# The attributes' bias added by VectorE, epsilon as a third triple of the statistics, a centred first matrix, spare rows by a maximum

## What is computed

```
h    = max(layernorm(x), 0)                       # eps 1e-5, no gamma
xn   = layernorm(h) * g1 + b1
msg  = relu(xn[src] + edge_attr)                  # one row per edge
aggr = segment_sum(msg, dst)                      # one row per node
u    = (1 + eps_gin) * xn + aggr
x2   = h + relu(u @ Wg1 + bg1) @ Wg2 + bg2
f    = gelu((layernorm(x2) * g2 + b2) @ Wf1 + bf1) @ Wf2 + bf2
out  = x + x2 + f
```

## Time and profile before

| | us |
|---|---|
| median of three runs | 1241.77 |
| profiled execution, its own time | 1243.35 |
| profiled execution, span | 1241.6 |
| busy: TensorE, VectorE, ScalarE, GpSimd | 1099.0, 1118.4, 999.1, 939.4 |
| same over 140 to 1150 us | 954.90, 968.17, 875.25, 814.47 |

### The profile page before, as it was taken

How to read it: one execution, slowest core, us unless ns; L and a number is a source line. 1 busy time by engine, 2 the same in 40 slices (tenths; PEclk the granted TensorE clock), 3 DMA queues, 4 the chain that set the end, 5 groups by cost and what they waited for, 6 DMA issues and landing times.

```text
span 1241.6 us, 28921 instructions
## 1 busy us (share of the span) xinstructions
PE 1099.0 (89%) x7264; PEld 921.0 (74%) x7264; DVE 1118.4 (90%) x5523; ACT 999.1 (80%) x2354; POOL 939.4 (76%) x698
## 2 busy tenths in 40 slices
PE   0257899999899999999899899999999999999988
PEld 0235688778788787788788787778778778787877
DVE  2888899999899999999899998999999999999842
ACT  0258789889888888989888888989889889979864
POOL 4488688878787887878787888888788788885630
PEclk9967999999999999999999999999999999999989
DMA  5879944444444444444444444544454454443220
GB/s 118 322 233 327 342 112 121 113 108 121 110 110 122 108 111 121 109 109 123 107 109 117 115 111 104 124 105 111 111 121 111 107 123 113 112 100 83 52 54 34
DMA packets 111491, 157.15 MB, mean 127 GB/s; under 512 B 24592, under 2 KB 51640, under 8 KB 111367
## 3 DMA queue, kind: packets, MB, share of 16 engines
q1 hardware_dynamic: 73606, 130.31, 32.8%
q0 software_dynamic: 37760, 25.66, 14.8%
HBM read 91.26 MB, written 64.61 MB: 126 GB/s over the span
## 4 chain that ended last, share of the span: by engine, by line
DVE 58%; issue 14%; POOL 11%; PE 9%; ACT 2%; DMA 1%; DVEq 1%; SPq 0%; ACTq 0%; POOLq 0%
DVE n_stat L635 12%; DVE n_mom L640 5%; DVE n_in L826 5%; POOL aggr_sums L480 5%; DVE e_stat L635 4%; DVE n_relu L645 4%; DVE e_match L740 4%; DVE n_out L833 3%; DVE n_x L811 3%; DVE n_zg L816 3%; DVE n_x2b L845 3%; PE p_f L892 3%; PE p_out L936 3%; POOL e_x L427 2%; DVE e_sum L798 2%
## 5 line engine op out<-in xcount | busy, mean ns | idle before, releaser
L480 POOL DMA_INDIRECT aggr_sums<-e_merged,e_index x196 | 326.5, 1666 | 81.9 <-issue 57.3
L936 PEld LDWEIGHTS p_out<-wf,n_act 128*128 128x128 f32 x3136 | 365.6, 192 | 3.5
L936 PE MATMUL p_out<-wf,n_act 128*128 128x128 f32 x3136 | 365.9, 275 | 0.0
L503 ACT ACTIVATE n_act<-p_f,bf1e_col 128x512 f32<-128x512 f32 x392 | 264.1, 674 | 18.1 <-PE p_f L892 17.5
L427 POOL DMA_INDIRECT e_x<-in_x,e_cols x196 | 216.4, 1104 | 71.9 <-issue 53.7
L494 ACT ACTIVATE n_z<-n_relu,n_shift,n_rstd 128x128 f32<-128x128 f32 x392 | 161.6, 483 | 127.9 <-DVE n_shift L664 127.4
L892 PE MATMUL p_f<-n_z2T_high,wf_low 128*128 128x512 f32 x392 | 190.6, 486 | 62.6 <-DVE n_z2T_low L678 35.9
L440 POOL TENSOR_TENSOR n_rstd<-n_var,minus_half 128x8 f32<-128x8 f32 x98 | 196.7, 2007 | 5.3 <-DVE n_var L657 5.3
L892 PEld LDWEIGHTS p_f<-n_z2T_high,wf_low 128*128 128x128 f32 x392 | 74.9, 191 | 164.0 <-ACT n_act L503 114.8
L446 POOL TENSOR_TENSOR n_rstd<-n_var,minus_half 128x4 f32<-128x4 f32 x98 | 103.5, 1056 | 119.8 <-DVE n_var L855 118.7
L635 DVE BATCH_NORM_STATS2 n_stat<-n_x 128x6 f32<-128x128 f32 (+1 forms) x784 | 168.9, 276 | 0.0
(11 more groups left out here) (91 smaller groups left out, 1997.3 us busy)
## 6 DMA issues: line engine op xcount, KB each, us to landing
n_x<-in_x SPq DMA_DIRECT2D x97, 256.0 KB, 2.9
n_aggr<-aggr_sums SPq DMA_DIRECT2D x97, 256.0 KB
out_dram<-n_out SPq DMA_DIRECT2D x97, 256.0 KB
aggr_sums<-zeros SPq DMA_DIRECT2D x13, 1024.0 KB, 8.3
e_dst<-in_dst_rows SPq DMA_DIRECT2D x49, 256.0 KB, 3.7
e_attr<-in_attr SPq DMA_DIRECT2D x48, 256.0 KB, 2.8
aggr_sums<-zeros SPq DMA_DIRECT2D x6, 2048.0 KB, 13.5
e_x<-in_x,e_cols POOLq DMA_INDIRECT x196, 2.8
```

Of the source, the lines that this page charges most:

```text
L480: nc.gpsimd.indirect_dma_start(out=aggr, out_offset=bass.IndirectOffsetOnAxis(ap=e_index[0:r, s, j:j + 1], axis=0), in_=e_merged[0:r, s, j ...
L503: nc.scalar.activation(n_act[:, k, :, 0:b.rows], p_f[k % 2][:, :, 0:b.rows], ACT.Gelu, bias=bf1e_col[:, k:k + 1]).then_inc(s_act, 1)
L936: last = nc.tensor.matmul(p_out[0:b.rows, j, :], n_act[:, k, j, 0:b.rows], wf2[:, k, :], start=False, stop=(k == KF - 1), skip_group_check ...
```

## The change

1. The addition of b1 to the attributes moves from GpSimd to VectorE (`add_b1`), behind the match matrix at the end of each step with half 0. SyncE's next load of attributes still waits for the same semaphore, now raised by VectorE.
2. The statistics' tiles have nine numbers for a row. The last three are a constant third triple (0, 0, 128 x 1e-5), written at the start by six memsets, so that `bn_aggr` over nine numbers gives the variance with 1e-5 in it. `first_variance` and `n_var2` go; `variance` writes into the moments, and GpSimd reads the moments with a step of two. Three of the five kinds of `bn_aggr` read nine numbers (the first and the third layernorm of a node, the first of an edge), two still read six.
3. Wf1 times g2 gets the mean over its 128 rows subtracted (one more matmul, one more VectorE subtraction, once), so the third layernorm no longer needs its mean: `shift2` goes, and ScalarE scales without a shift.
4. `e_toward` goes: `e_extra` is the spare row or 0, and `e_index` is the maximum of it and the destination.

```
                 if (b := node(1)) is not None:
-                    nc.gpsimd.tensor_tensor(n_rstd[0:r, s], n_var[0:r, s],
+                    nc.gpsimd.tensor_tensor(n_rstd[0:r, s], n_mom[0:r, s, :, :, 1],
...
                 if (b := node(4)) is not None:
-                    pool.wait_ge(s_var2, b.at + 1)
-                    nc.gpsimd.tensor_tensor(n_rstd2[0:r, s], n_var2[0:r, s], minus_half[0:r, 0:J],
+                    pool.wait_ge(s_mom2, b.at + 1)
+                    nc.gpsimd.tensor_tensor(n_rstd2[0:r, s], n_mom2[0:r, s, :, 1], minus_half[0:r, 0:J],
                                             ALU.pow).then_inc(s_rstd2, 1)
                 if 0 in halves and (c := edge(2)) is not None:
-                    if c.is_number(0):
-                        pool.wait_ge(s_edge_param, 16 * len(EDGE_PARAMS))
-                    pool.wait_ge(q_attr[s], 16 * (c.uses(3) + 1))
-                    reached(pool, s_esum, c.at - 2)
-                    nc.gpsimd.tensor_tensor(e_attrb[0:r, s], e_attr[0:r, s], b1_row[0:r],
-                                            ALU.add).then_inc(s_eattrb, 1)
                     pool.wait_ge(s_evar, c.at + 1)
-                    nc.gpsimd.tensor_tensor(e_rstd[0:r, s], e_var[0:r, s, 1], minus_half[0:r, 0:J],
+                    nc.gpsimd.tensor_tensor(e_rstd[0:r, s], e_mom[0:r, s, 1, :, 1], minus_half[0:r, 0:J],
                                             ALU.pow).then_inc(s_erstd, 1)
...
                 if (b := node(4)) is not None:
-                    act.wait_ge(s_shift2, b.at + 1)
+                    r = b.rows
+                    act.wait_ge(s_rstd2, b.at + 1)
                     reached(act, s_tz2, b.at - 1)
-                    per_row(n_z2[:, b.slot(2)], n_x2[:, b.slot(3)], n_rstd2[:, b.slot(6)],
-                            n_shift2[:, b.slot(6)], b.rows).then_inc(s_z2, 1)
+                    for j in range(J):
+                        last = nc.scalar.activation(n_z2[0:r, b.slot(2), j, :], n_x2[0:r, b.slot(3), j, :],
+                                                    ACT.Identity, scale=n_rstd2[0:r, b.slot(6), j:j + 1])
+                    last.then_inc(s_z2, 1)
...
+            nc.vector.memset(mean_of[:], 1.0 / D).then_inc(s_ones, 1)
+            for of in (e_stat[:, :, 0], n_stat[:, :, 0], n_stat2[:]):
+                nc.vector.memset(of[:, :, :, 6:8], 0.0).then_inc(s_stat_eps, 1)
+                nc.vector.memset(of[:, :, :, 8:9], EPS * D).then_inc(s_stat_eps, 1)
...
+                dve.wait_ge(s_wf1, 1)
+                dve.wait_ge(s_wf1_mean, 1)
+                nc.vector.tensor_tensor(wf1g[:], wf1g[:], p_f[1][:].rearrange("p j q -> p (j q)"),
+                                        ALU.subtract).then_inc(s_wf1, 1)
+                dve.wait_ge(s_wf1, 2)
+                nc.vector.tensor_copy(wf1_high[:], wf1g[:]).then_inc(s_wf1, 1)
                 dve.wait_ge(s_b1g, 1)
-                dve.wait_ge(s_wf1, 2)
+                dve.wait_ge(s_wf1, 3)
                 nc.vector.tensor_tensor(wf1_low[:], wf1g[:], wf1_high[:], ALU.subtract).then_inc(s_wf1, 1)
                 dve.wait_ge(s_b2f, 1)
...
-            def moments(to, of, rows, done):
+            def moments(to, of, width, rows, done):
+
                 for j in range(J):
-                    last = nc.vector.bn_aggr(to[0:rows, j, :], of[0:rows, j, :])
+                    last = nc.vector.bn_aggr(to[0:rows, j, :], of[0:rows, j, 0:width])
                 last.then_inc(done, 1)
...
-            def first_variance(var, mom, rows, done):
-
-                nc.vector.tensor_scalar(var[0:rows, 0, :], mom[0:rows, 0, :, 1], EPS, None, ALU.add).then_inc(done, 1)
-
-            def second_variance(var, mom, rows, first, at, done):
-
-
-                dve.wait_ge(first, at + 1)
-                nc.vector.scalar_tensor_tensor(var[0:rows, 1, :], var[0:rows, 0, :], EPS,
+            def variance(mom, rows, done):
+
+                nc.vector.scalar_tensor_tensor(mom[0:rows, 1, :, 1], mom[0:rows, 0, :, 1], EPS,
                                                mom[0:rows, 1, :, 1], ALU.mult, ALU.add).then_inc(done, 1)
 
...
-            def shift2(node):
-                if (b := node(4)) is not None:
-                    r, s = b.rows, b.slot(6)
-                    dve.wait_ge(s_rstd2, b.at + 1)
-                    nc.vector.scalar_tensor_tensor(n_shift2[0:r, s], n_mom2[0:r, s, :, 0], -1.0, n_rstd2[0:r, s],
-                                                   ALU.mult, ALU.mult).then_inc(s_shift2, 1)
...
                     dve.wait_ge(s_estat, c.at + 1)
                     nc.vector.tensor_copy(e_dstf[0:r, s], e_cols[0:r, s, 1, :]).then_inc(s_ecopy, 1)
-                    moments(e_mom[:, s, 0], e_stat[:, s, 0], r, s_emom)
-
-                    dve.wait_ge(s_ecopy, c.at + 1)
-                    nc.vector.tensor_tensor(e_toward[0:r, s], spare[0:r], e_dstf[0:r, s],
-                                            ALU.subtract).then_inc(s_etoward, 1)
+                    moments(e_mom[:, s, 0], e_stat[:, s, 0], STAT, r, s_emom)
                     dve.wait_ge(s_emom, c.at + 1)
...
                     shift(node)
-                shift2(node)
                 z2_low(node)
-                first_variance_of(node)
                 if c is not None:
 
 
                     dve.wait_ge(q_dst[s], 16 * (c.uses(3) + 1))
+                    dve.wait_ge(s_ecopy, c.at + 1)
...
-                second_variance_of(node)
+                variance_of(node)
+
+            def add_b1(c):
+
+                if c is not None:
+                    r, s = c.rows, c.slot(3)
+                    if c.is_number(0):
+                        dve.wait_ge(s_edge_param, 16 * len(EDGE_PARAMS))
+                    dve.wait_ge(q_attr[s], 16 * (c.uses(3) + 1))
+                    reached(dve, s_esum, c.at - 2)
+                    nc.vector.tensor_tensor(e_attrb[0:r, s], e_attr[0:r, s], b1_row[0:r],
+                                            ALU.add).then_inc(s_eattrb, 1)
...
-                    nc.vector.scalar_tensor_tensor(e_extra[0:r, s], e_count[0:r, s], 1.5, e_toward[0:r, s],
+                    nc.vector.scalar_tensor_tensor(e_extra[0:r, s], e_count[0:r, s], 1.5, spare[0:r],
                                                    ALU.is_gt, ALU.mult).then_inc(s_eextra, 1)
-                    moments(e_mom[:, s, 1], e_stat[:, s, 1], r, s_emomu)
+                    moments(e_mom[:, s, 1], e_stat[:, s, 1], 6, r, s_emomu)
                     relu_moments(node)
                     if not (c.fixed and c.k < 3):
                         dve.wait_ge(q_scatter[s], SCATTERED * c.uses(3))
                     dve.wait_ge(s_eextra, c.at + 1)
                     nc.vector.tensor_tensor(e_index[0:r, s], e_dstf[0:r, s], e_extra[0:r, s],
-                                            ALU.add).then_inc(s_eindex, 1)
-                    dve.wait_ge(s_emomu, c.at + 1)
-                    first_variance(e_var[:, s], e_mom[:, s], r, s_evar0)
+                                            ALU.max).then_inc(s_eindex, 1)
...
                     relu_moments(node)
-                shift2(node)
                 z2_low(node)
-                first_variance_of(node)
                 if c is not None:
-                    second_variance(e_var[:, s], e_mom[:, s], r, s_evar0, c.at, s_evar)
-                second_variance_of(node)
+                    dve.wait_ge(s_emomu, c.at + 1)
+                    variance(e_mom[:, s], r, s_evar)
+                variance_of(node)
                 if ending is not None:
...
-                    moments(n_mom[:, b.slot(6), 0], n_stat[:, b.slot(6), 0], b.rows, s_nmom)
+                    moments(n_mom[:, b.slot(6), 0], n_stat[:, b.slot(6), 0], STAT, b.rows, s_nmom)
                 if (b := fifth) is not None:
                     r, s = b.rows, b.slot(6)
                     dve.wait_ge(s_stat2, b.at + 1)
                     nc.vector.tensor_tensor(n_x2b[0:r, s], n_x2[0:r, b.slot(3)], n_x[0:r, s],
                                             ALU.add).then_inc(s_x2b, 1)
-                    moments(n_mom2[:, s], n_stat2[:, s], r, s_mom2)
...
-                if (b := fifth) is not None:
-                    r, s = b.rows, b.slot(6)
-                    dve.wait_ge(s_mom2, b.at + 1)
-                    nc.vector.tensor_scalar(n_var2[0:r, s], n_mom2[0:r, s, :, 1], EPS, None,
-                                            ALU.add).then_inc(s_var2, 1)
                 if 0 in halves or not halves:
                     first_half(edge(1), node)
+                    if 0 in halves:
+                        add_b1(edge(2))
                 if 1 in halves:
                     second_half(edge(1), edge(2), node)
...
+            pe.wait_ge(s_wf1, 1)
+            pe.wait_ge(s_ones, 3)
+            nc.tensor.matmul(p_f[1][:], mean_of[:], wf1g[:], start=True, stop=True).then_inc(s_wf1_mean, 1)
             pe.wait_ge(s_bias, 1)
-            pe.wait_ge(s_wf1, 3)
+            pe.wait_ge(s_wf1, 4)
```

(22 more changed lines are left out.)

34 lines of the change are left out of this document (15 added, 19 removed).

## The result

The changed kernel takes 1193.67 us as the median of four runs (1191.93 to 1194.49), the kernel before 1241.97 (1239.85 to 1242.43) beside it. The profiled execution took 1193.22 us (before 1243.35), so 50.1 us are to be found in the two traces.

The account below looks back on a forecast made before the run. VectorE was taken as the bound, busy 968.2 of 1010 us in the middle; -26.0 + 29.4 + 3.1 - 21.7 - 3.0 - 2.4 = -20.6 us, from 1243.35 to 1222.8, stated as 1222; own ends 1208 and 1236, range up to 1240.

Parts of the forecast that it names:

- small instructions removed: VectorE, per node block and edge chunk: dropping short shifts, epsilon additions and variances saves 20.6 + 5.4 us, -26.0 in all.
- the addition on VectorE: End of the step: adding b1 on VectorE costs 0.60 us in each of 49 chunks, +29.4 us.
- wider moments: 980 bn_aggr instructions reading nine numbers for six, at 1.0 ns a number: +3 us, ends 0 and +34.
- `n_in` no longer stopped: Edge-free node addition on VectorE: GpSimd's b1 addition no longer blocks it, (895 - 674) ns x 98 = -21.7 us.
- the branch: Loop turn on VectorE: the addition before it covers up to 0.52 us of 12 gaps; half taken, -3 us.
- the start: Before 140 us: the chain of waits passes through GpSimd's b1 addition twice, 1.10 and 1.29 us, saving 2.4 us.
- both gaps: VectorE idle once a loop pass, before `n_x2` (14.5 us) and `n_zg` (16.4 us), read as its sequencer coming round.
- The port: SBUF access shared by VectorE and GpSimd: `e_attrb` stops two-input VectorE additions, powers do not; freeing it gains 21.7 us.
- rival (b): `n_in` and the new addition: powers block them instead, so 1244.5 us, or 1256 if the addition is stopped too; chance 0.07.
- Rival (a): Small VectorE instructions were free or TensorE takes over: half the 26.0 and no branch gain, 1239, or 1233; chance 0.15.
- Rival (d): More gained: `e_toward` counts fully and the branch is covered, 1214, or 1208 with lower ends; chance 0.73 including the forecast.

## Why the prediction was wrong

The direction, the forecast's mechanism and most terms held. The size did not, and one step has most of it.

| term | predicted | shown |
|---|---|---|
| small instructions removed | -26.0 | about -26 by starts at the same distances, less by the time: see below |
| the addition on VectorE | +29.4 | +29.4: 707 ns, next start 0.60 to 0.65, none stopped |
| wider moments | +3.1 | none clear of the noise; 3 ns a moment by starts |
| `n_in` no longer stopped | -21.7 | (895 - 673) x 98 = -21.8 |
| the branch | -3 (0 to -6) | 30.9 to 5.7 of idle time: -25.2 |
| the start | -2.4 | first `n_in` at 67.4 for 69.4: -2.0 |
| sum | -20.6 | -45.6; measured -50.1 |

**The step that failed is the branch.** I read both gaps rightly as VectorE's sequencer coming round the loop, and then let the change act only on the first of them: "If the sequencer goes round while the engine still adds, up to 0.60 - 0.08 us of each of 12 gaps is covered, 6 us; if not, 0." Coverage turned out full and more (1.40 to 0.63 us a turn on the mean, 11 turns and not 12: -8.5 us in the count of lost time). The second gap I left as a constant of the loop, when it is a property of where the body begins: it held 17.4 us before and nothing after. My range had no case for it: every end I gave was a cost of an operation. Without a loop the two kernels lie 30.6 us apart, with it 48.3, so 17.7 us of the gain belong to the turn and its place. The order of the instructions was there to be counted; a gap between the first and a later instruction of a loop's body, with no producer late, asked for it. It was luck, too, that the other edits moved the body to a good place: with 26 instructions more ahead of the loop the same change would have gained 5.9 us.

**The port: right in the trace, wrong as a model.** `n_in` fell by 21.8 us, as forecast. Powers stop nobody: 42 of the 98 `n_in` and 66 of the 98 `n_x2b` overlap one in the changed kernel, 63 of these `n_x2b` lie wholly inside it, and none takes over 693 ns. So rival (b) falls, though the new addition itself (at most 0.73 us) met a power only twice. But I took the 21.7 us as a fixed tax. It is a meeting of two engines in time: it was 22.6 us before (29 long `n_in`, each 1.40 to 1.46 us), 31.0 once the loop's gaps were gone, 53.0 with the rest of the change alone in the loop, 63.2 without it. Each time VectorE was made faster and GpSimd's addition left in place, the stops ate a part of it (8.4 of the 33 us of the gaps) or all of it and more (the small instructions). The two halves of the change are thus worth more together than apart: without the loop -12.5 and +10.1 alone, -30.6 together.

**The small instructions.** Their price is to be had only beside the moved addition: -18.1 us without the loop (1206.84 to 1188.74), where the sum has -26.0 + 3.1 = -22.9. Some of what went had stood in front of a wait: the count of lost time rises by 8.3 us between these two kernels (10.1 to 18.4), 4.7 of it before `e_minus`. With the addition left on GpSimd the same edits gave +10.1 without the loop and -0.2 with it. `e_toward` was worth next to nothing, as forecast: `e_minus` starts 0.43 us behind the first moment for 0.41, now waiting for it. Rival (a) had the right suspicion (what is removed may not be gained) and the wrong place: TensorE does not take over. Its size of half is not borne out either beside the moved addition. Rival (d), more than forecast because the branch is covered, was the nearest, and at 1214 still 20 us off. Its lower end adds up to 1209 rather than 1208, and the forecast's upper one to 1235 rather than 1236; neither matters here.

**Not accounted for:** 4.5 us of the 50.1. They lie at the end. From the start to `n_in` 20 the rows give -7.4 us (measured 301.8 to 293.8, -8.0); from there to `n_in` 80 they give -36.4 (704.1 to 668.8, -35.3); from there to the last `n_in`, where no turn of the loop leaves a gap, they give -2.4 (four stops of 0.75 less, eight or nine additions, +5.1, the small ones, -4.5) and 192.0 to 185.3, -6.7, was measured. The addition may cost less than 0.60 where VectorE is not alone the bound; no row shows it.

## What to carry to other kernels

A gap just behind a loop's branch is a cost of code placement, and any edit ahead of the loop can buy or sell it (here up to 42 us of 1240): count the body's first instruction and the packets of the instruction queue before crediting an edit, and try a few idle instructions ahead of the loop, or the loop written out, as the control. A stop at the shared port is not a tax to be subtracted; it depends on what meets what, so an edit that speeds up VectorE can be paid back there, and moving the colliding instruction should be tried together with it. And once an engine is 98% busy, look at what it waits for from itself: an order with the need one or two instructions further behind its producer was worth 11 us here.
